# Layer 0's routed experts in blocks of 128 rows, in four strands that share loaded weights

## The reference

```python
B, S, D, F, E, SH, K = (2, 512, 512, 256, 16, 2, 2)
def _experts_all(x, g, gb, w1, b1, w2, b2):
    y = gelu(einsum('bsd,edf->bsef', x, g) + gb)          # exact erf
    y = y * (einsum('bsd,edf->bsef', x, w1) + b1)
    return einsum('bsef,efd->bsed', y, w2) + b2
aff = sigmoid(x @ wa);  topk_p, topk_i = top_k(aff, K)     # 2 of 16 experts a token
topk_p = topk_p / sum(topk_p)
routed = sum over the chosen experts, weighted by topk_p
shared = sum of the two shared experts;  return x + shared + routed
```

## Time and profile before

| what | value |
|---|---|
| median of 3 runs | 1644.98 us (1644.34 to 1646.87) |
| the profiled execution | 1644.98 us, its span 1643.2 us |
| busy in the span | PE 1401.9, DVE 1062.4, ACT 698.8, POOL 612.8 us |
| the routed stage of layer 0 | 419.96 to 732.58 us |
| mean granted TensorE clock | 0.919 |

### The profile page before, as it was taken

One profiled execution on the slowest core, in us unless ns is written; L12 is line 12 of the kernel. 1 busy time (PEld: TensorE's weight loads), 2 busy tenths in 40 slices (PEclk: granted clock), 3 DMA queues, 4 the chain that ended last, 5 costly groups with the idle time before them and its releaser, 6 DMA issues. The chain is left out here.

```text
span 1643.2 us, 23435 instructions
## 1 busy us (share of the span) xinstructions
PE 1401.9 (85%) x8186; PEld 1196.2 (73%) x8186; DVE 1062.4 (65%) x1837; ACT 698.8 (43%) x1123; POOL 612.8 (37%) x607
## 2 busy tenths in 40 slices
PE   6999769999699999963899879998598899999960
PEld 5787657776599999952799868887466777777750
DVE  4688746234467767645787456775474688888857
ACT  4121032000366565631455444442332288888850
POOL 1455500000322222214465423333036377777734
PEclk8999979999799999995999979997699799999995
DMA  4000040000688888843210000000321899999958
GB/s 161 1 1 26 27 131 0 1 1 0 208 272 292 273 280 283 277 145 115 65 52 14 1 33 2 27 27 27 110 100 51 318 343 341 347 345 345 347 131 306
DMA packets 112519, 239.25 MB, mean 146 GB/s; under 512 B 13481, under 2 KB 48297, under 8 KB 112443
## 3 DMA queue, kind: packets, MB, share of 16 engines
q1 hardware_dynamic: 84699, 169.55, 29.5%
q0 software_dynamic: 18784, 51.39, 11.3%
q10 hardware_dynamic: 8960, 17.30, 2.7%
HBM read 187.49 MB, written 50.72 MB: 145 GB/s over the span
## 5 line engine op out<-in xcount | busy, mean ns | idle before, releaser
L1049 POOL COPY e_index<-r_token_of 128x2 int32 (+1 forms) x31 | 7.9, 255 | 368.9 <-POOLq L602 202.5
L66 PE MATMUL bank<-e_xt_hi,e_w_hi 128*128 128x256 f32 x496 | 142.8, 288 | 0.0
L68 PE MATMUL bank<-e_xt_hi,e_w_lo 128*128 128x256 f32 x496 | 140.2, 283 | 0.0
L67 PE MATMUL bank<-e_xt_lo,e_w_hi 128*128 128x256 f32 x496 | 140.1, 282 | 0.0
L2421 POOL DMA_INDIRECT sums<-e_y,r_target_of x64 | 110.2, 1721 | 68.2 <-DMA sums<-e_y,r_target_of 41.1
L1150 DVE TENSOR_TENSOR e_w_lo<-e_raw,e_w_hi 128x2048 fp32r<-128x2048 f32 x31 | 71.1, 2292 | 84.9 <-ACT e_w_hi L1107 84.9
L2531 DVE TENSOR_TENSOR e_w_lo<-r_w_early,e_w_hi 128x1536 fp32r<-128x1536 f32 x48 | 84.6, 1763 | 24.3 <-ACT e_w_hi L2495 22.6
L66 PEld LDWEIGHTS bank<-e_xt_hi,e_w_hi 128*128 128x128 f32 x496 | 94.1, 190 | 0.0
L67 PEld LDWEIGHTS bank<-e_xt_lo,e_w_hi 128*128 128x128 f32 x496 | 94.1, 190 | 0.0
L68 PEld LDWEIGHTS bank<-e_xt_hi,e_w_lo 128*128 128x128 f32 x496 | 94.0, 189 | 0.0
L66 PE MATMUL bank<-e_w_hi,e_xt_hi 128*96 128x384 f32 x256 | 90.3, 353 | 3.4 <-DVE e_w_lo L2531 3.4
(11 more groups left out here) (464 smaller groups left out, 4720.8 us busy)
## 6 DMA issues: line engine op xcount, KB each, us to landing
r_w_early<-in_w_gate_up SPq DMA_DIRECT2D x48, 768.0 KB
e_raw<-in_rw SPq DMA_DIRECT2D x62, 512.0 KB
r_w_early<-in_w_down SPq DMA_DIRECT2D x24, 768.0 KB
e_raw<-in_rg SPq DMA_DIRECT2D x31, 512.0 KB
results<-e_y ACTq DMA_DIRECT2D x31, 512.0 KB, 5.3
rows<-resid SPq DMA_DIRECT2D x8, 1024.0 KB, 4.3
r_w_first<-in_w_gate_up SPq DMA_DIRECT2D x8, 768.0 KB
e_w_raw<-in_w_down SPq DMA_DIRECT2D x8, 768.0 KB
```

The lines of the kernel that those rows point to most:

```text
L66: pe.matmul(out, a_hi, b_hi, start=start, stop=False)
L67: pe.matmul(out, a_hi, b_lo, start=False, stop=False)
L68: return pe.matmul(out, a_lo, b_hi, start=False, stop=stop)
```

## The change

A group becomes a block of 128 rows (`GRP` = P), so there are `NG0` = 32 + 15 = 47 blocks; a 48th column exists in the tables. Four buffers ("strands", `U0` = 4) are filled so that strand p has the blocks 12p to 12p+11 of the sorted order, one in every fourth step. So successive blocks of a strand mostly have the same expert. The weights of one block are one indirect DMA of 128 rows of 12 KB (gate, up and down of one partition beside one another in `w_expert0`); where the block has the same expert as the one ahead of it in its strand, all 128 indices are put beyond the bound, and nothing is moved (`load_of`). With 16 experts and 4 strands that leaves at most 19 blocks with a load. High and low parts are made anew for every block.

The products change to tokens stationary, weights moving: gate and up are one group of 12 matmuls of 512 columns (256 of gate, 256 of up) and one more for both biases: a stationary one-hot (`expert_here`) against a table of all biases, high parts in rows 0 to 15, low parts in rows 32 to 47. The hidden rows are then turned on TensorE (2 transposes). Down's low part moves from VectorE to GpSimd, the copy of the results from ScalarE to VectorE, the store from ScalarE's queue to SP's. In the tables `group_expert` and `group_bias` go and `load_of` and `expert_here` come; the column tables shrink from 62 to 48 columns.

The tables (cut):

```diff
-GRP = 256
+GRP = P
 NG0 = (2 * T) // GRP + E0 - 1
+NGA = NG0 + 1
+U0 = 4
+NH0 = NGA // U0
@@ columns
-  step(vec.tensor_tensor(at_col[:, :, :], iota_s[:, :].unsqueeze(1).to_broadcast([P, 2 * NT, 2 * NG0]),
+  step(vec.tensor_tensor(at_col[:, :, :], iota_g[:, :].unsqueeze(1).to_broadcast([P, 2 * NT, NGA]),
@@ group_tables
-  for a, table in enumerate((rgb, rub)):
-      for f in range(FB):
...
-          step(vec.tensor_reduce(k.group_bias[:, :, 2 * a + f], gprod[:, :, :], AX.X, ALU.add))
+  step(vec.tensor_scalar(part_e[:, :], part[:, :], 32.0, -32.0, ALU.is_ge, ALU.mult))
+  step(vec.tensor_tensor(part_e[:, :], part[:, :], part_e[:, :], ALU.add))
+  step(vec.tensor_scalar(load_f[:, :], gef[:, :], float(P), part[:, 0:1], ALU.mult, ALU.add))
+  step(vec.tensor_tensor(same[:, 1:NG0], gef[:, 1:NG0], gef[:, 0:NG0 - 1], ALU.is_equal))
+  step(vec.tensor_scalar(k.expert_here[:, 0:NG0], gef[:, :], part_e[:, 0:1], None, ALU.is_equal))
+  step(vec.memset(same[:, :].rearrange("p (a b) -> p a b", b=NH0)[:, :, 0:1], 0.0))
+  step(vec.scalar_tensor_tensor(k.load_of[:, 0:NG0], same[:, 0:NG0], float(E0 * P), load_f[:, :], ALU.mult, ALU.add))
```

The routed stage, where all loops are new (the removed ones are printed above):

```diff
+  store(h, p), on SP:
+      sp.wait_ge(s_ysb, U * h + p + 1)
+      sp.dma_start(y_rows[bass.ds(NH0 * p + h, 1)].rearrange("g p d -> p (g d)"), y[p][:, :]).then_inc(s_y[p], 16)
+  rows(h, p), on GpSimd:
+      if h:
+          pool.wait_ge(s_g[p], 16 * h)
+          pool.wait_ge(s_tps, U * (h - 1) + p + 1)
+      c = NH0 * p + h
+      pool.indirect_dma_start(xg[p][:, :], None, k.rows, bass.IndirectOffsetOnAxis(k.token_of[:, c:c + 1], 0)).then_inc(s_g[p], 16)
+  weights(h, p), on GpSimd:
+      if h:
+          pool.wait_ge(s_w[p], 16 * h)
+          pool.wait_ge(s_wlo, U * (h - 1) + p + 1)
+          pool.wait_ge(s_vlo, U * (h - 1) + p + 1)
+      pool.indirect_dma_start(raw[p][:, :], None, io["w_expert0"], bass.IndirectOffsetOnAxis(k.load_of[:, c:c + 1], 0),
+                              bounds_check=E0 * P - 1, oob_is_err=False).then_inc(s_w[p], 16)
+  down_lo(h, p), on GpSimd:
+      pool.wait_ge(s_vhi, U * h + p + 1)
+      pool.tensor_tensor(w2_lo[p][:, :], w2_raw[p], w2_hi[p][:, :].bitcast(F32), ALU.subtract).then_inc(s_vlo, 1)
+  weights(0, 0); rows(0, 0); pool.memset(b1 ...); then weights(0, p), rows(0, p) for p in 1..3
+  for g in range(U, NG0 + U):
+      if g < NG0:
+          rows(g // U, g % U)
+      down_lo(g // U - 1, g % U)
+      if g < NG0:
+          weights(g // U, g % U)
+  on TensorE:
+  gate_up: for b in range(KD):
+      mm3(pe, out, xt_hi[p][:, t], xt_lo[p][:, t], w1_hi[p][:, c], w1_lo[p][:, c], b == 0, False)
+  pe.matmul(out, k.expert_here[:, NH0 * p + h:NH0 * p + h + 1].to_broadcast([P, P]), b1[:, :], start=False, stop=True)
+  for g in range(-1, NG0 + 1):
+      for stage, item in ((turn, g + 1), (turn_hidden, g - 1), (gate_up, g), (down, g - 1)):
+          if 0 <= item < NG0:
+              stage(item // U, item % U)
+  on ScalarE (gelu first makes w2_hi of the same block, then waits for gate_up):
+  three_stages(act, NG0, turned_hi, gelu, nothing, between=hidden_hi, prepare=weights_hi, unroll=U)
+  on VectorE (hidden: ge times up's half of the bank; results: copy of down's bank to y):
+  three_stages(vec, NG0, turned_lo, hidden, results, between=hidden_lo, prepare=weights_lo, unroll=U)
```

More of the change, by code:

```diff
@@ L993, in experts0_routed @@
     nc, bank, io = k.nc, k.bank, k.io
-    FB, S = F0 // P, GRP // P
-    W = KD * F0
+    FB = F0 // P
+    U = U0
     with ExitStack() as ctx:
[L997 to L1020, removed]
@@ new lines, in experts0_routed @@
+        two = lambda name, shape, dt=F32: [k.sb(f"e0_{name}{p}", shape, dt, ctx) for p in range(2)] * 2
+        four = lambda name, shape, dt=F32: [k.sb(f"e0_{name}{p}", shape, dt, ctx) for p in range(U)]
+        W1 = KD * 2 * F0
+        raw = four("raw", [P, W1 + FB * D])
+        w1_raw, w2_raw = [r[:, 0:W1] for r in raw], [r[:, W1:] for r in raw]
+        w1_hi, w1_lo = two("w1_hi", [P, KD * 2 * F0], F32R), two("w1_lo", [P, KD * 2 * F0], F32R)
+        w2_hi, w2_lo = two("w2_hi", [P, FB * D], F32R), two("w2_lo", [P, FB * D], F32R)
@@ new lines, in experts0_routed @@
+        b1_raw, b1_hi = k.sb("e0_b1_raw", [P, 2 * F0], F32, ctx), k.sb("e0_b1_hi", [P, 2 * F0], F32R, ctx)
+        b1 = k.sb("e0_b1", [P, 2 * F0], F32R, ctx)
+        xg = four("xg", [P, D])
+        xt_hi, xt_lo = two("xt_hi", [P, KD * P], F32R), two("xt_lo", [P, KD * P], F32R)
+        ge, hf = two("ge", [P, F0]), two("hf", [P, F0])
+        ht_hi, ht_lo = two("ht_hi", [P, FB * P], F32R), two("ht_lo", [P, FB * P], F32R)
+        y = four("y", [P, D])
+        each = lambda name: [k.sem(f"e0_{name}{p}") for p in range(U)]
@@ L1026, in _ @@
             def _(sp):
[L1027 to L1038, removed]
@@ L1040, in _, with store @@
-                three_stages(sp, NG0, load, nothing, nothing)
+                for r in (0, 32):
+                    sp.dma_start(b1_raw[r:r + E0, :], io["b1"]).then_inc(s_b1, 16)
+                def store(h, p):
+                    sp.wait_ge(s_ysb, U * h + p + 1)
+                    sp.dma_start(y_rows[bass.ds(NH0 * p + h, 1)].rearrange("g p d -> p (g d)"), y[p][:, :]).then_inc(s_y[p], 16)
+                three_stages(sp, NG0, nothing, nothing, store, unroll=U)
+                for p in range(U):
+                    sp.wait_ge(s_y[p], 16 * ((NG0 + U - 1 - p) // U))
@@ L1083, in gate_up @@
-                    mm.then_inc(s_gu, 1)
+                    out = bank[2 + p % 2][:, :]
+                    for b in range(KD):
+                        t, c = slice(b * P, (b + 1) * P), slice(b * 2 * F0, (b + 1) * 2 * F0)
+                        mm3(pe, out, xt_hi[p][:, t], xt_lo[p][:, t], w1_hi[p][:, c], w1_lo[p][:, c], b == 0, False)
+                    pe.matmul(out, k.expert_here[:, NH0 * p + h:NH0 * p + h + 1].to_broadcast([P, P]), b1[:, :], start=False, stop=True).then_inc(s_gu, 1)
```

242 lines of the change are left out of this document (114 added, 128 removed).

## The result

The changed kernel takes **1663.51 us** (median of 4 runs, 1662.63 to 1665.02); the kernel before, on the same chip, 1644.91 us (4 runs, 1644.34 to 1646.87). The ratio is 1.0112 with a 95% interval of 1.0094 to 1.0129: 1.1% slower, a small difference but clear of the noise. The forecast was 1665.

A forecast was written before the change was run, and what follows sets the result against it. TensorE's column stream bounded the kernel before; after the change, a VectorE-GpSimd exclusion circle of 6.7 us a block. Stage +20.7, tables -1.2: 1645 + 20.7 - 1.2 = 1664.5, say 1665 us; range 1632 to 1692.

The forecast's parts named there:

- The circle: Layer 0's routed experts: VectorE's and GpSimd's subtractions exclude one another, load and gather between; 6.7 us a block.
- the load's tail: On GpSimd: a load asked for during VectorE's two-input subtraction ends 0.81 us behind that subtraction's end.
- GpSimd's 5.0 us: GpSimd's work per block, 2.4 + 2 x 1.25 + 0.1: it would fit if independent of VectorE.
- The chain of 5.4: ScalarE and VectorE per block: turn, high part, weights' high part, low part, product sum to 5.4 us, above TensorE's 5.0.
- first rival: No exclusion in practice in layer 0's experts: cadence is the chain's 5.4 us, time 1608 us; chance 0.17.
- TensorE's idle time: In the stage's blocks: TensorE idles 1.7 of 6.7 us, before the turn of hidden rows.
- The beginning and the end: Stage borders: first gate and up 435.2, last 740.1, then 3.0 + 10.2 to the end at 753.3, +20.7 us.
- The tables: Ahead of the stage: column tables shrink to 1.72 and 1.8 us, so 1.2 of TensorE's 1.57 us wait comes back.
- Unknown (1), skipped loads: Loads skipping all 128 rows: full 0.81 us assumed; nearly free would give 1645 us, chance 0.13.
- (2), rows of 12 KB: Load with 12 KB rows: 0.95 us to perhaps three times it; then cadence about 7, +13 us.
- (3): Down's low part on GpSimd at 1.5 or 2.9 us instead of 2.4: 5.8 or 7.2 a block, -39 or +21.
- Late weights: Loads land 0.4 us before ScalarE's copy; rival: 2.5 us slower or clock falls, 1696 us; chance 0.15 with clock.

The follow-up runs named there:

- e1: Changed kernel with down's low part back on VectorE, behind the hidden product: 1605.31 us, ratio 0.9761 to the kernel before.
- e2: Changed kernel without the loads after the first four, later blocks computing with those weights: 1602.52 us (one run).
- e3: Changed kernel with two GpSimd memsets of 128x1024 in place of its subtraction, down's high-by-low product left out: 1605.9 us (one run).
- e4: Changed kernel with all 47 blocks really loading their weights, nothing skipped: 1662.64 us.
- e9: Changed kernel with down's low part on VectorE, the results' copy on ScalarE and the weights' parts made two blocks ahead: 1609.8 us.
- e10: Changed kernel with half of down's low part on GpSimd, half on VectorE behind the hidden product: 1650.54 us, ratio 1.0043 to the kernel before.
- e8: Kernel before with only down's low part moved to GpSimd, in the second stage of its loop: 1836.67 us, ratio 1.1161.

## Why the prediction was right

- **The circle.** Predicted 0.81 + 0.30 + 0.95 + 0.05 + 2.4 + 2.16 = 6.7 us; in the timeline 0.90 + 0.30 + 0.96 + 0.03 + 2.40 + 2.16 = 6.75. The one term off in it is the load's tail, taken from a row gather of the earlier trace rows. A sum beside it was off too: GpSimd's 5.0 us counts 0.30 of issue ahead of each DMA, but ahead of the load the profile shows 0.90, so its order needs 5.6, more than the chain. In the circle that costs nothing, because the load has to wait for VectorE anyway. GpSimd's 128x1024, worked out from two smaller shapes of the earlier trace rows, came to the number. e1, e2 and e3 each cut the circle and each gave the chain's 5.4.
- **The chain of 5.4** was a by-product of the prediction (first rival, 1608 us). Its terms add up to 5.34, which was carried on as 5.4; e1 has 5.38 and 1605. (The 0.54 us quoted there for TensorE's wait in layer 1 is that of its weight load; the matmul's own row shows 0.36.)
- **TensorE's idle time** was forecast as 1.7 us a block, ahead of the turn of the hidden rows. The profile shows 49.9 us in 39 blocks, 1.3 each, and the larger part of it, 0.87, ahead of down: that down waits for GpSimd's low part was in no step of the forecast.
- **The beginning and the end.** First gate and up 435.06 (435.2 predicted), last one 740.04 (740.1). Inside, two small errors cancel: 41 intervals average 6.75, not 43 of 6.7, and the other five are 5.4 to 6.0. The load lands as forecast: TensorE turns the first rows at 428.85. From the end of the last gate and up (the gelu at 743.31) to the next stage 10.6, for 10.2.
- **The tables.** 1.75 and 1.83 us, for 1.72 and 1.8; TensorE's wait of 1.57 fell to 0.55. Of the 1.2 forecast 1.0 came there, and 0.5 of it is left at the stage's border (the last residual add starts at 418.43 instead of 418.96). So by the forecast's steps the next stage would begin at 753.3 - 1.2 = 752.1; it begins at 753.95. The 1.3 that the later stages are shorter, which no step foresaw, hides most of that: the profiled execution took 1665.0, the sum was 1664.5. That the two are as close as half a microsecond is luck.
- **Unknown (1), skipped loads:** the full price, as taken (e4: all 47 loads, same time). **(2), rows of 12 KB:** 1.00 us for one issue, hardly more than a gather's 0.95. **(3):** 2.40.
- **Late weights:** no wait for the weights' DMA, and a clock of 1.00. The margin of 0.4 us was right: in e4, where every block loads, a load lands 8.8 us after its issue begins (median), and the copy that needs the load of 565.21 starts 9.2 later, at 574.44. e4 shows two short waits, e9 what comes when the weights are wanted a block earlier.
- **The skill's sentences.** "SBUF — State Buffer", section "Who interferes with whom", of the Trainium skill: that a VectorE instruction with two SBUF inputs and a GpSimd one that reads SBUF exclude one another agrees with the runs in both orders (VectorE 2.16 behind GpSimd's end here, GpSimd 2.26 behind VectorE's in e2). Which of them goes first is not always the one that asked first: VectorE's half in e10 had asked 0.6 earlier and ended last. Its inference that descriptors can be made in VectorE's hold does not: the load asked for at 565.21 ends 0.90 behind the hold instead of after 1.00. Had it held, the forecast's first rival would not quite have come either: GpSimd's own order of 5.6 a block would have set the pace, 1605 + 41 x 0.21, some 1614 us by an estimate from e1's time and the rows above.

## What to carry to other kernels

Before an operation is moved to GpSimd to relieve VectorE, list on one time line every instruction of VectorE with two SBUF operands and every indirect DMA and SBUF-reading instruction of GpSimd, and follow who asks in whose hold around a whole block: GpSimd's sum of 5.0 us (5.6 with the idle time that it left out) said that it would nearly fit, the circle said 6.7. Look in the same way at what stands behind the moved instruction in its new queue: a gather behind it cost most of 193 us (e8), a load behind it closed the circle. And when one wait is cut, the next is near: the experiments that halved the operation or reordered the chain met a new one at once.

## What was not expected of the hardware

- Two writes of 128x1024 on GpSimd inside VectorE's hold took 0.96 and 0.95 us: a pure write isn't held up, as e3's theory had it, while an indirect DMA's issue is (a gather takes 2.53 in e1, 0.96 free; a load 2.52 in e9, 1.00 free).
- An indirect DMA of 128 rows of 12 KB is issued in 1.00 us, one of 2 KB rows in 0.95, and one with all indices out of bounds takes as long as one that moves 1.5 MB.
- A load that waits for a low part starts 0.90 us behind that part's end, whether GpSimd made it (here and in e3) or VectorE (0.89 in e1, 0.90 in e10), where a row gather behind another DMA shows 0.30. Why wasn't looked into.
